# A cross network over 128 tiles: batches of two tiles, or one tile at a time

## What is computed

```python
def step(x, wb):
    wi, bi = wb
    xw = jnp.matmul(x, wi)          # (16384, 4096) @ (4096, 1)
    x_new = x0 * xw + bi + x
    return (x_new, None)
x, _ = jax.lax.scan(step, inputs, (w, b))   # six layers
```

## Time and profile before

| | |
|---|---|
| median of 3 runs | 1285.65 us (1285.22 to 1285.83) |
| profiled execution, its own time | 1286.89 us |
| its span, first to last instruction | 1285.0 us |
| busy: TensorE matmul, weight load | 785.6 us (61%), 734.8 us (57%) |
| busy: VectorE, ScalarE, GpSimd | 1150.7 us (90%), 95.9 us (7%), 7.3 us (1%) |
| granted TensorE clock, mean | 0.774 |
| moved by DMA | 537.69 MB, mean 418 GB/s over the span |

### The profile page before, as it was taken

How to read it: one execution, slowest core, us unless ns; L and a number is a source line. 1 busy time by engine, 2 the same in 40 slices (tenths; PEclk the granted TensorE clock), 3 DMA queues, 4 the chain that set the end, 5 groups by cost and what they waited for, 6 DMA issues and landing times.

```text
span 1285.0 us, 19296 instructions
## 1 busy us (share of the span) xinstructions
PE 785.6 (61%) x8724; PEld 734.8 (57%) x8724; DVE 1150.7 (90%) x529; ACT 95.9 (7%) x324; POOL 7.3 (1%) x32
## 2 busy tenths in 40 slices
PE   6666665655665566566566556556656656656554
PEld 3666565655555565565566555556656655556553
DVE  5999998988988989889888898898988988989887
ACT  1000000000000000000000000000000000000000
POOL 2000000000000000000000000000000000000000
PEclk9887777778777777778767787877877777777776
DMA  9999999999999999999999999999999999999996
GB/s 310 418 426 429 429 429 430 429 429 430 429 429 429 431 430 429 419 425 426 423 420 413 423 425 424 424 425 425 426 422 423 424 425 424 422 423 423 426 413 277
DMA packets 38025, 537.69 MB, mean 418 GB/s; under 512 B 4255, under 2 KB 4447, under 8 KB 5471
## 3 DMA queue, kind: packets, MB, share of 16 engines
q1 hardware_dynamic: 18716, 269.13, 50.6%
q10 hardware_dynamic: 19296, 268.44, 49.0%
HBM read 269.12 MB, written 268.44 MB: 418 GB/s over the span
## 4 chain that ended last, share of the span: by engine, by line
DMA 79%; DVE 10%; PE 8%; ACT 1%; issue 1%; SPq 0%; DVEq 0%
DMA out_dram<-tiles 60%; DMA tiles<-in_r_inputs_dram 19%; PE dots L322 8%; DVE tiles L264 6%; DVE blocks L251 4%; ACT spread L182 1%; DVE tiles L286 1%; DVE tiles L216 0%; SPq L127 0%; DVEq L43 0%; SPq L122 0%; PE turned L336 0%; DVE scale L258 0%; ACT growth L189 0%; DVEq L250 0%
## 5 line engine op out<-in xcount | busy, mean ns | idle before, releaser
L322 PE MATMUL dots<-blocks,weights 128*64 128x128 f32 x8192 | 701.8, 351 | 395.9 <-DVE blocks L251 395.1
L322 PEld LDWEIGHTS dots<-blocks,weights 128*64 128x64 f32 x8192 | 666.9, 187 | 421.0 <-DVE blocks L251 420.1
L251 DVE STREAM_TRANSPOSE blocks<-tiles 128x2048 f32<-128x2048 f32 x252 | 567.1, 2289 | 113.9 <-issue 109.2
L264 DVE SCALAR_TENSOR_TENSOR tiles<-tiles,scale,c_last 128x4096 f32<-128x4096 f32 x126 | 562.5, 4464 | 0.0
L182 ACT ACTIVATE spread<-dots,group_mask 128x128 f32<-128x128 f32 x256 | 73.2, 369 | 1073.7 <-PE dots L322 1057.1
L336 PE MATMUL turned<-layer_sel,spread 128*128 128x8 f32 x512 | 67.8, 259 | 79.6 <-ACT spread L182 79.6
L336 PEld LDWEIGHTS turned<-layer_sel,spread 128*128 128x128 f32 x512 | 62.0, 191 | 95.1 <-ACT spread L182 95.1
L189 ACT ACTIVATE growth<-turned,ones 128x16 f32<-128x16 f32 x64 | 17.6, 274 | 80.7 <-PE turned L336 56.3
L223 DVE STREAM_TRANSPOSE blocks<-tiles 128x1024 f32<-128x1024 f32 x8 | 9.2, 1211 | 8.6 <-DMA tiles<-in_r_inputs_dram 8.6
L258 DVE TENSOR_TENSOR_SCAN scale<-growth,cw 128x6 f32<-128x6 f32 x128 | 13.1, 142 | 2.9 <-ACT growth L189 2.9
L304 PE MATMUL scratch<-tiles,ones 6*128 6x512 f32 x16 | 14.4, 1076 | 2.0 <-ACT c_last L173 2.0
(11 more groups left out here) (18 smaller groups left out, 5.3 us busy)
## 6 DMA issues: line engine op xcount, KB each, us to landing
tiles<-in_r_inputs_dram SPq DMA_DIRECT2D x128, 2048.0 KB, 14.9
out_dram<-tiles ACTq DMA_DIRECT2D x126, 2048.0 KB, 25.5
out_dram<-tiles ACTq DMA_DIRECT2D x8, 512.0 KB, 3.8
tiles<-in_L_rec_w_dram SPq DMA_DIRECT2D x4, 96.0 KB
strips_b<-in_L_rec_b_dram SPq DMA_DIRECT2D x1, 96.0 KB, 1.9
strips_w<-in_L_rec_w_dram SPq DMA_DIRECT2D x1, 96.0 KB, 2.1
tiles<-in_L_rec_b_dram SPq DMA_DIRECT2D x1, 96.0 KB
```

Source lines behind the costliest of these rows:

```text
L251: nc.vector.transpose(blocks[:, c, :, :].rearrange("p t n -> p (t n)"), tiles[:, at:at + TB, c * CH:(c + 1) * CH]).then_inc(blocks_ready, 1)
L264: nc.vector.scalar_tensor_tensor(out=tiles[:, s, :], in0=tiles[:, s, :], scalar=scale[:, batch % 2, t, L - 1:L], in1=c_last[:], op0=ALU.mu ...
L322: last = nc.tensor.matmul(dots[at:at + KM * Q, :, :, :], weights[:, c * KB + k:c * KB + k + KM, :], blocks[:, c, :, k * Q:(k + KM) * Q], s ...
```

## The change

A batch becomes one tile: `TB` is 1, and `BR` 8 so that there are still eight slots. There are 128 batches. The columns are cut in two chunks of 2048 (`NCHUNK = 2`), so a transpose still is one instruction of 128x2048, now 2048 columns of one tile. VectorE transposes both chunks of tile n, then scans and finishes tile n - 1. `blocks` is half as large. A dots matmul moves 64 columns, those of one tile, and there are 64 matmuls per tile. ScalarE makes the copies of tile n, issues the store of tile n - 1, then makes growth. The last tile alone is finished in four pieces. All other loops follow from the constants.

```diff
--- before.py
+++ after.py
@@ -10,10 +10,10 @@
 P = 128
 Q = 32
 G = P // Q
-TB = 2
-BR = 4
+TB = 1
+BR = 8
 KM = 2
-NCHUNK = 4
+NCHUNK = 2
 LP = 8
 BANK = 512
 HALF_BANKS = 4
@@ -196,9 +196,8 @@
             spread_dots(0)
             make_growth(0)
             for batch in range(1, n_batches):
-                store((batch - 1) * TB)
                 spread_dots(batch)
-                store((batch - 1) * TB + 1)
+                store(batch - 1)
                 make_growth(batch)
 
             for n in range(TB * PIECES):
@@ -268,14 +267,12 @@
             for batch in range(1, n_batches):
                 for n in range(batch * TB, (batch + 1) * TB):
                     dve.wait_ge(x_landed[n % n_slots], (n // n_slots + 1) * 16)
-                transpose_chunks(batch, range(0, NCHUNK // 2))
+                transpose_chunks(batch, range(NCHUNK))
                 if batch == 1:
                     dve.wait_ge(scratch_copied, n_halves)
                     dve.wait_ge(cw_ready, 1)
                 scan(batch - 1)
                 finish(batch - 1, 0)
-                transpose_chunks(batch, range(NCHUNK // 2, NCHUNK))
-                finish(batch - 1, 1)
             scan(n_batches - 1)
 
             dve.wait_ge(scale_ready, n_tiles)
```

## The result

The kernel after the change takes 1305.47 us (median of 4 runs, 1305.29 to 1307.05), the one before 1285.43 us beside it. The ratio is 1.0154, 95% interval 1.0143 to 1.0166: 20 us more, where I had forecast 1.8 us less.

A forecast was written before the change was run, and what follows sets the result against it. It took one late DMA engine of sixteen to bound the kernel, with compute hidden and the start worth zero. The tail's 1.8 us came off the 1285.0 us span, giving 1283.2 and a median of 1283.8 us; range 1280.0 to 1287.5.

The forecast's parts named there:

- the late engine: Whole loop: one DMA engine of sixteen lags and sets the pace, 9.90 us per tile, with unchanged work.
- the doubled small instructions on ScalarE: Loop: 64 more rounds of copies, at most 91 us in all on a mostly idle engine, so free.
- the one that ended slower: Rival, chance 0.06: matmul pairs get no cheaper with fewer columns, TensorE becomes the bound, 1680 us.
- VectorE: Loop: 9.0 us of work per tile against the DMA pace of 9.90, so 0.9 us spare.
- TensorE: Loop: cost per pair goes with columns, 0.055 us at full clock, at most 0.11; round at most 8.8 us, hidden.
- Order and waits: Loop: growth is ready two to three us before the next scan wants it, so VectorE doesn't wait for it.
- Stores: Loop: time from a store's issue to landing rises from 25.5 to 44 us, while loads stay at 14.9.
- The circuit of eight slots: Loop: eight slots at 9.90 us make 79.2 us; what compute gives up, the stores' queue takes.
- Start: Start: first store comes earlier, at 37 us, behind loads that keep the DMAs busy; gain zero.
- Tail: Tail: last stores and pieces land in even steps of about 5.1 us per tile; 1.8 us saved, bounds 0 and 2.5.
- the hole in the tail: Tail, before the change: the late engine stood empty for 1.75 us before store 125; the change was to fill this.
- The rival of the deeper store queue: Rival, chance 0.12: more outstanding stores keep the faster engines at 429 GB/s, saving 9 us, 1276 us.

The follow-up runs named there:

- a_half_pe: The kernel after the change with half of the dots matmuls left out: 1282.83 us, 0.9973 of the kernel before.
- b_split: The kernel before, still in batches of two tiles, with each dots matmul split into two of 64 columns: 1303.05 us, ratio 1.0132.
- a_hold: The kernel after the change with each store issued two tiles later: 1312.21 us, 1.0194 of the kernel before.
- a_pool: The kernel after the change with 13056 added GpSimd instructions, waits on a long-set semaphore and their loop: 1321.78 us, 1.0273 of the kernel before.

## Why the prediction was wrong

The step that failed is in its first part: "Its work is the same bytes before and after. What counts is where it stands empty." The bytes are the same, but the late engine's time for them is not fixed. It went from 9.90 to 10.10 us per tile with nearly twice the instructions, and no step of the sum had a term for that. I priced the doubled matmuls on TensorE and the doubled small instructions on ScalarE ("free") by these engines' own time, and never asked what 17207 more instructions do to the one resource I had named as the bound. The 16384 instructions between a_half_pe and the kernel after cost 23.3 us (0.0181 x 1285.4); less the 3.5 us by which a_half_pe is under the kernel before, that is 19.8 us slower, as measured. (b_split, in which the same instructions cost 17 us, shows that this price isn't fixed.) None of the rivals had it: the one that ended slower put the cost of more instructions on TensorE too.

What held, by the prediction's own steps. One tile of the loop after the change:

```profile
609.29 4.50 DVE L250 STREAM_TRANSPOSE blocks<-tiles 128x2048 f32<-128x2048 f32 x2 [0.94 <-DMA tiles<-in_r_inputs_dram]
...
611.65 6.61 PE L319 MATMUL dots<-blocks,weights 128*64 128x64 f32 x128 [1.87 <-DVE blocks L250]
613.72 0.13 DVE L257 TENSOR_TENSOR_SCAN scale<-growth,cw 128x6 f32<-128x6 f32 x1
613.88 4.49 DVE L263 SCALAR_TENSOR_TENSOR tiles<-tiles,scale,c_last 128x4096 f32<-128x4096 f32 x1
618.31 0.31 ACT L182 ACTIVATE spread<-dots,group_mask 128x64 f32<-128x64 f32 x1 [8.22 <-PE dots L319]
618.40 0.34 ACTq L194 DMA_DIRECT2D out_dram<-tiles  x1
...
619.29 0.61 PE L333 MATMUL turned<-layer_sel,spread 128*128 128x8 f32 x4 [1.03 <-ACT spread L182]
619.32 4.50 DVE L250 STREAM_TRANSPOSE blocks<-tiles 128x2048 f32<-128x2048 f32 x2 [0.96 <-DMA tiles<-in_r_inputs_dram]
```

- VectorE: 9.1 us of work per tile (609.29 to 618.37) for 9.0 forecast, and 0.95 us idle, now put down to the landing of a load. Right.
- TensorE: its 128 records take 6.61 us, (6.61 - 0.3) / 63.5 = 0.10 us per pair at a mean clock of 0.55, for at most 0.11. In the start, at full clock:

```profile
33.24 3.95 PE L319 MATMUL dots<-blocks,weights 128*64 128x64 f32 x128
```

  (3.95 - 0.2) / 63.5 = 0.059 us for 0.055. The cost does go with the columns. Right. (The Trainium skill, "TensorE: Matmul & The Clock Gate", section "Wait — 56ns, not 53.3ns?", has 62 ns per MATMUL where the sequencer's code decodes them; two in 59 ns show that this isn't the case here.)
- Order and waits: growth comes at 620.2, 3.5 us before the next scan at 623.75. No wait for growth but one, of 1.7 us, after the loop. Right.
- Stores: 40.0 us to landing for 44 forecast, and loads 21.4 for "14.9 as now". The circuit of eight slots had to hold what compute gave up; I put all of it into the stores' queue, and a part went to the loads'. It cost nothing: a_hold, with the short queue, is no faster in pace.
- Start: the first store is issued at 38.6 us for 37. Right. Whether it gains anything is not told apart (see the tail).
- Tail: the steps are even and the hole is gone. The size was off: the batch of one gives 3.5 us (a_half_pe), not 1.8; a_half_pe has 823 more instructions than before, so it may be 4.5. Where the other 2 to 3 us come from, the start or the tail, no run separates. So the forecast's one term, the hole in the tail, has not been measured by itself.

The rival of the deeper store queue was wrong: a_half_pe has 36.6 us from a store's issue to its landing, for 25.5, and its pace is 9.90 us, as before.

## What to carry to other kernels

In a kernel bound by the DMAs, count the executed instructions of all engines, and not only what each costs on its own engine: here a thousand more, on TensorE or GpSimd, cost 1.0 to 1.5 us of 1285, even where they touched no data and ran on an idle engine (in executions that were recorded, as all here were), and doubling them cost more than the shorter batch gave. Where the windows of a tail show a DMA share of one sixteenth, the pace is probably that of one late DMA engine: read it from the spacing of the loads that wait for stores, since the mean GB/s doesn't show it. And to halve a unit of work, look for a form that doesn't double its instructions; the gain of the shorter unit (0.27%, measured with half of the matmuls left out) comes only then. Where fewer, wider instructions delay the first store, look at the DMA share of the start, too: what they save can go there.

## What the runs showed of the hardware that was not expected

- Instructions on an idle engine that read and write nothing slow the DMA: 13057 waits on GpSimd added 1.42% (1.19 to 1.64), spread evenly while they ran, and added up with TensorE's (a_pool, 1321.78 us for 1322 expected).
- The cost seems to fall first on one DMA engine of sixteen: up to 400 us all together moved 425 to 431 GB/s, as before, while the loads already went at 10.11 us for 9.86, and at the end that one worked on alone for 9 us.
- Half of what TensorE reads made no difference to it: half the moving columns 0.9991, half the weight columns 0.9989, half the matmuls 0.9915.
- The DMA queues show no fetching anew of a loop's instructions: 13 packets on the instruction queues with 19296 executed instructions and with 32353.
- Where the first store comes late, the DMAs run dry once at the start: some 8.6 us empty between 40 and 80 us in a_hold, which takes 7 us longer than the kernel after the change.
